# Two value products summed in one 32-row group, and row maxima written by GpSimd's DMAs, in a two-layer decoder kernel

## The reference

```
scores = jnp.einsum('bhqd,bhkd->bhqk', q, k) / np.sqrt(D).astype(np.float32)
scores = scores + bias[None]
scores = jnp.where(mask[None, None], scores, -jnp.inf)
wei = jax.nn.softmax(scores, axis=-1)
return jnp.einsum('bhqk,bhkd->bhqd', wei, v)
```

## Time and profile before

| | |
|---|---|
| median of 3 runs | 711.33 us (709.43 to 711.8) |
| profiled execution | 705.17 us, span 703.4 us |
| TensorE busy | 605.9 us, 86% |
| DVE, ACT, GpSimd busy | 562.7, 500.7, 319.2 us |
| chain that ended last | TensorE 55%, DVE 21%, issue 8%, GpSimd 6% |

### The profile page before, as it was taken

How to read it: one execution, slowest core, us unless ns; L and a number is a source line. 1 busy time by engine, 2 the same in 40 slices (tenths; PEclk the granted TensorE clock), 3 DMA queues, 4 the chain that set the end, 5 groups by cost and what they waited for, 6 DMA issues and landing times.

```text
span 703.4 us, 20504 instructions
## 1 busy us (share of the span) xinstructions
PE 605.9 (86%) x7396; PEld 362.6 (52%) x7396; DVE 562.7 (80%) x1551; ACT 500.7 (71%) x1229; POOL 319.2 (45%) x536
## 2 busy tenths in 40 slices
PE   0589899676677879999999989899999999999994
PEld 0256566444456658655454444455555555545663
DVE  5689988899999996878787777677777677678885
ACT  3689999977778746688888775577776766765531
POOL 3336765797899979865655311111211211101110
PEclk9999999988999989999999999999999999999998
DMA  6686974221111002444434426344354344330011
GB/s 229 142 170 157 251 114 85 53 66 46 38 39 38 32 3 40 76 77 78 77 76 78 82 59 104 70 86 76 62 92 78 61 92 77 54 52 19 32 38 38
DMA packets 162308, 55.18 MB, mean 78 GB/s; under 512 B 148448, under 2 KB 160032, under 8 KB 161952
## 3 DMA queue, kind: packets, MB, share of 16 engines
q1 hardware_dynamic: 162208, 53.88, 37.8%
HBM read 16.89 MB, written 5.24 MB: 31 GB/s over the span
## 4 chain that ended last, share of the span: by engine, by line
PE 55%; DVE 21%; issue 8%; POOL 6%; ACT 4%; DMA 4%; SPq 2%; DVEq 0%; ACTq 0%; POOLq 0%
PE bank L1330 5%; PE bank L1278 4%; PE bank L1264 3%; PE bank L999 3%; DVE l_neg_max L568 3%; PE bank L1679 3%; PE bank L1285 3%; DVE mix_num_den L1543 2%; PE bank L1303 2%; PE bank L1020 2%; DVE l1x_neg_max L1178 2%; PE bank L974 2%; PE bank L961 2%; PE bank L1356 2%; PE bank L1335 2%
## 5 line engine op out<-in xcount | busy, mean ns | idle before, releaser
L1178 DVE TENSOR_REDUCE l1x_neg_max<-bank 128x2 f16<-128x448 f32 (+1 forms) x192 | 116.0, 639 | 39.2 <-PE bank L1285 38.3
L1233 ACT ACTIVATE l1x_probs<-bank 128x512 f32<-128x512 f32 x192 | 104.3, 593 | 32.9 <-PE bank L1307 22.6
L886 DVE TENSOR_REDUCE l1a_neg_max<-bank 128x4 f16<-128x512 f32 x128 | 83.5, 676 | 18.8 <-PE bank L974 17.3
L934 ACT ACTIVATE l1a_probs<-bank 128x512 f32<-128x512 f32 x128 | 69.4, 593 | 18.2 <-PE bank L988 18.2
L1125 POOL TENSOR_TENSOR l1x_rstd<-l1x_var_eps,minus_half 128x1 f32<-128x1 f32 x16 | 8.8, 550 | 135.8 <-DVE l1x_var_eps L1154 135.8
L1679 PE MATMUL bank<-mix_xT_parts,w_ternary 128*128 128x256 f16 x384 | 49.9, 280 | 12.2 <-DVE mix_hidden L1561 11.6
L1679 PEld LDWEIGHTS bank<-mix_xT_parts,w_ternary 128*128 128x128 f16 x384 | 36.4, 100 | 24.6 <-DVE mix_hidden L1561 15.8
L568 DVE TENSOR_REDUCE l_neg_max<-bank 128x4 f16<-128x512 f32 x64 | 41.8, 674 | 4.7 <-PE bank L697 4.3
L1493 POOL TENSOR_TENSOR mix_hidden_parts<-mix_hidden,mix_hidden_parts 128x256 f16<-128x256 f32 x48 | 38.4, 810 | 6.0 <-ACT mix_hidden_parts L1624 5.8
L1751 POOL TENSOR_TENSOR moe_rstd<-moe_var_eps,minus_half 128x1 f32<-128x1 f32 x16 | 8.8, 549 | 62.6 <-DVE moe_var_eps L1769 62.6
L1624 ACT CAST mix_hidden_parts<-mix_hidden 128x256 f16<-128x256 f32 x48 | 19.2, 406 | 25.1 <-DVE mix_hidden L1561 25.0
(11 more groups left out here) (265 smaller groups left out, 1797.8 us busy)
## 6 DMA issues: line engine op xcount, KB each, us to landing
ctx_projected<-mix_ctx_projected SPq DMA_DIRECT2D x16, 192.0 KB, 2.0
l1x_ctx_projected<-ctx_projected SPq DMA_DIRECT2D x16, 160.0 KB, 2.5
...
```

Source lines behind the costliest of these rows:

```text
L886: dve.tensor_reduce(mm[:, 16 * j + 4 * s:16 * j + 4 * s + 4], b_s[c % 3][:].rearrange("p (r k) -> p r k", k=P), AX.X, ALU.max, negate=True ...
L934: act.activation(prob[:, c, :], b_st[c % 2][:], ACT.Exp).then_inc(s_exp, 1)
L1178: dve.tensor_reduce(mm[:, first:first + count], scores, AX.X, ALU.max, negate=True).then_inc(s_max, 1)
L1233: act.activation(prob[:, c, :], b_st[c % 2][:], ACT.Exp).then_inc(s_exp, 1)
```

## The change

In l1a and l1x the second value product of a block (c = 1) takes its 32 weight columns 16 columns earlier. The columns of each kv head are 8 values, a one and zeros, so with that shift the product leaves rows 0 to 15 of a group as they are and adds values and sum in rows 16 to 24. Both products thus accumulate in one bank: the first starts it, the second ends it. OE, T1 and T1b run once a block instead of twice; the reciprocal takes 32 elements a partition instead of 16, the product 256 instead of 128. The ring of copies has 2 slots instead of 4.

```diff
@@ l1x, TensorE (l1a alike)
             elif piece == "PV":
-                wait(pe, s_oe, b * 2 + c)
+                wait(pe, s_oe, b)
                 for x in range(4):
-                    pe.matmul(b_ot[32 * x:32 * x + 32, :], vs[:, b % 3, 4 * c + x, 0:32], prob[:, 6 * c + x, :],
-                              start=True, stop=False, skip_group_check=True)
+                    col = 64 * (4 * c + x) - 16 * c
+                    pe.matmul(b_ot[32 * x:32 * x + 32, :], v_flat[:, b % 3, col:col + 32], prob[:, 6 * c + x, :],
+                              start=c == 0, stop=False, skip_group_check=True)
             elif piece == "T1":
-                pe.wait_ge(s_oe, b * 2 + c + 1)
+                pe.wait_ge(s_oe, b + 1)
                 for r in range(4):
-                    ins = pe.transpose(b_tail[:, P * r:P * r + P], ots[:, 2 * bp + c, P * r:P * r + P], net.ident[:])
+                    ins = pe.transpose(b_tail[:, P * r:P * r + P], ots[:, bp, P * r:P * r + P], net.ident[:])
@@ ACT
             elif piece == "OE":
-                act.wait_ge(s_pv, b * 2 + c + 1)
-                act.copy(ots[:, 2 * bp + c, :], b_ot[:]).then_inc(s_oe, 1)
+                act.wait_ge(s_pv, 2 * (b + 1))
+                act.copy(ots[:, bp, :], b_ot[:]).then_inc(s_oe, 1)
```

In l1x the four DMAs of M move from SP's program to GpSimd's:

```diff
@@ sp_program
-            if piece == "M":
-                sp.wait_ge(s_mt, b + 1)
...
-                        sp.dma_start(dst, mt[r0:r0 + 8, :]).then_inc(s_md, 16)
@@ pool_program
+            elif piece == "M":
+                pool.wait_ge(s_mt, b + 1)
+                for j in range(2):
+                    for z in range(2):
+                        row, r0 = 64 * j + MROW, 16 * j + 8 * z
+                        dst = qt[row:row + 1, b % 3, :, 64 * z:64 * z + 64].rearrange("o (x u) q -> o x u q", u=2)
+                        pool.dma_start(dst, mt[r0:r0 + 8, :]).then_inc(s_md, 16)
```

The order tables are new in all five stages. For l1x on TensorE:

```diff
-        F5 S.4-2 T1.1-4 ST.2-3 S.5-2 F7 T4-4 ST.3-3 M-2 T5-4 S.0-1 ST.4-3 PV.0-3 ST.5-3 S.1-1 T1.0-3 S.2-1 ST.0-2
-        PV.1-3 S.3-1 ST.1-2"""),
+        S.4-2 F5 T1.0-4 S.5-2 ST.2-3 T4-4 F7 M-2 ST.3-3 T5-4 S.0-1 ST.4-3 PV.0-3 S.1-1 ST.5-3 S.2-1 ST.0-2 S.3-1
+        PV.1-3 ST.1-2"""),
```

More of the change, by code:

```diff
@@ L1234, in act_program @@
             elif piece == "OE":
-                act.wait_ge(s_pv, b * 2 + c + 1)
-                wait(act, s_t1, (b - 2) * 2 + c + 1)
-                act.copy(ots[:, 2 * bp + c, :], b_ot[:]).then_inc(s_oe, 1)
+                act.wait_ge(s_pv, 2 * (b + 1))
+                wait(act, s_t1, b - 1)
+                act.copy(ots[:, bp, :], b_ot[:]).then_inc(s_oe, 1)
             elif piece == "T4":
@@ L1334, in pe_program @@
                     late = prob[:, 6 * c + 4 + x % 2, 256 * (x // 2):256 * (x // 2) + 256]
-                    ins = pe.matmul(out, vs[:, b % 3, 4 * c + x, 32:64], late.rearrange("p (r q) -> p r q", r=4),
-                                    start=False, stop=True, skip_group_check=True)
+                    col = 64 * (4 * c + x) - 16 * c + 32
+                    ins = pe.matmul(out, v_flat[:, b % 3, col:col + 32], late.rearrange("p (r q) -> p r q", r=4),
+                                    start=False, stop=c == 1, skip_group_check=True)
                 ins.then_inc(s_pv, 1)
             elif piece == "T1":
-                pe.wait_ge(s_oe, b * 2 + c + 1)
-                wait(pe, s_t2, b * 4 + 2 * c)
-                if b == 0 and c == 0:
+                pe.wait_ge(s_oe, b + 1)
+                wait(pe, s_t2, 2 * b)
+                if b == 0:
                     take(pe, prev.left, 0)
-                if c == 0:
-                    wait(pe, s_x, b)
+                wait(pe, s_x, b)
                 for r in range(4):
-                    ins = pe.transpose(b_tail[:, P * r:P * r + P], ots[:, 2 * bp + c, P * r:P * r + P], net.ident[:])
+                    ins = pe.transpose(b_tail[:, P * r:P * r + P], ots[:, bp, P * r:P * r + P], net.ident[:])
                 ins.then_inc(s_t1, 1)
             elif piece == "T4":
-                pe.wait_ge(s_t2, 4 * (b + 1))
+                pe.wait_ge(s_t2, 2 * (b + 1))
                 for a in range(2):
```

178 lines of the change are left out of this document (96 added, 82 removed), and 19 rows, old and new, of the table TIMES.

## The result

| | before | after |
|---|---|---|
| median of 4 runs | 711.57 us (709.43 to 712.43) | 702.11 us (700.82 to 702.93) |
| profiled execution | 705.17 us, span 703.4 us | 701.63 us, span 699.8 us |
| TensorE busy | 605.9 us | 592.3 us |

A forecast was written before the change was run, and what follows sets the result against it. TensorE looked like the bound in l1a and l1x, but loops with DVE and ACT would turn its savings into waits. Terms 0 (l0, mix), 0 (l1a), -3.5 (overlaps), 0 (l1x), 0 (GpSimd) gave 707.8 us, band 703 to 712.

The forecast's parts named there:

- l1x: l1x alone: the removed T1 comes back as waits, net about 0, from -10 to +5 us over 12 blocks.
- The wait ahead of S.2: l1x on TensorE: 0.4 us waiting for DVE's reduction in place of T1, besides 0.59 us ahead of ST.0.
- 0 for l1a alone: l1a alone, ten blocks: no gain, from -6 to +2 us.
- the walk of the turn: One l1a block followed on ACT and DVE from M: closes at 8.35 us against 8.32 before.
- Overlaps: Where two stages overlap: two thirds of 5.4 us of freed transposes gained, -3.5 us, from 0 to -7.
- GpSimd's transfers: l1x maxima issued by GpSimd: 1.0 us for each of four, hidden, so price 0.
- The limit that was worked out: l1x, GpSimd's time per issue that stays hidden: up to 1.2 us for ST.0, 1.12 for the low parts.
- Rival B: GpSimd's transfers hold up ST.0 and the next transposes in l1x: at 1.4 us each, 724 us; chance 0.2.
- Rival A: l1a and l1x: TensorE's whole saving of 20.5 us shows, 691 us; chance 0.2.
- Rival C: The new order of mix is worse: +8 us, with the overlaps 716 us; chance 0.15.
- Rival D: l1a and l1x: second value products held until earlier ones drain, 3.2 us more, 711 us; counted within the forecast's band.
- the first stages: l0 and mix, work kept but pieces shuffled: 0, from -4 to +6 us.

The follow-up runs named there:

- the first two experiments: Changed kernel with four unused extra transposes a block in l1x: between ST.5 and S.2, 702.89 us; behind PV.1, 707.3 us.
- the fourth: Kernel before with the value products summed in one bank, but the order tables of before and maxima by SP: 710.41 us, ratio to before 1.0031.
- T1 twice: Changed kernel with the four transposes of T1 in l1a done twice: 704.93 us.
- the third kernel: Changed kernel with the four transfers of l1x's maxima issued by SP again instead of GpSimd: 701.73 us.
- eight issues: Changed kernel with the four transfers of l1x's maxima cut into eight of half the size, all issued by GpSimd: 720.86 us.
- the nine kernels: The changed kernel and the follow-ups that keep its new tables in l0, mix and l1a; last addition of mix between 298.76 and 302.22 us.

## Why the prediction was right or wrong

**l1x: right, and shown.** The turn stayed at 13.36 us, S.2 and ST.0 came where they were walked, and the first two experiments and the fourth show that the removed transposes were nearly free. The wait ahead of S.2 came in its size; the one ahead of ST.0 is 0.34 us and not 0.6, because the walk let S.2 end 0.40 us after its start, and its rows last 0.57 us. The busy share fell to 95%, not to 92%: TensorE's busy time fell by 3.9 us in twelve turns, 0.32 us each, and not by 12 x 0.64; that the neighbours overlap a T1 group, so that it counts for 0.45 us, makes up some 0.19 of these 0.32 us. The wait of 0.48 us ahead of M was missed. That the sum of the turn came out all the same is in that part luck.

**l1a: the step that failed.** It stands as "0 for l1a alone" and "the turn closes at 8.35 us". Measured were 8.04 us, and -3.6 us over eleven turns in the pair of profiles. Counted from M at 347.34 us in the changed kernel, ST.3 came at 2.48 us (walked 2.6), ST.0 at 4.14 (4.25), ST.1 at 5.71 (5.85), S.3 at 5.94 (6.15) and the next M at 8.04 (8.35). The step is the walk of the turn, a sum of small errors to one side, 0.12, 0.07 and 0.10 us among them, each for a gap that was taken to be there, and together they ate the whole gain. The claim that DVE has no gap from 3.3 to 8.27 us is wrong too: it idles 0.21 and 0.22 us ahead of two of its reductions. T1 twice shows what the walk had not seen: in the new order T1 and F7 fill the time from S.3 to M on TensorE, and there the removed group is worth 0.42 us a turn. In the old order leaving out a T1, with its OE and the split of DVE's work, costs 0.15 us (8.31 to 8.46 us). So what the change brought in l1a came with the new order, for which the sum had no gain.

**Overlaps: too large, and not shown.** Forecast -3.5 us, in the pair of profiles -2.2 and +0.7, so -1.5 us; and the -2.2 us did not come again in the third kernel. A gain at the overlaps is not shown.

**GpSimd's transfers: right, with the wrong price.** The issue took 0.58 us and not 1.0, and lay below SP's, which was used as the lower bound; the term of the sum stays 0. By the Trainium skill ("DMA: Bandwidth & Descriptors", section "Latency and other measured facts") software-generated transfers begin 0.4 us later; here they land after 2.0 us in the median, and SP's transfers of l1a's maxima, of twice the size, after 1.7 us, which agrees in direction. The limit that was worked out, 1.1 to 1.2 us for each of four, agrees with what eight issues show, but a delay at the limit is not hidden: it cost 19 us. Rival B, with its 1.4 us, is ruled out in this kernel, but its mechanism exists. **Rival A** falls: its turns of 12.5 and 7.7 us stand against 13.36 and 8.04. **Rival C**, a worse order of mix, shows its sign in the pair of profiles, for the first addition of l1a came at 318.36 us and not at 316.78. But in the nine kernels with that order it came between 315.05 and 318.41 us, at 316.5 in the mean, so the order of mix is not worse. **Rival D** falls: 256 products of L1330 took 604 ns each before and 605 after, and l1x kept its turn.

**The time.** The direction is right and the size is too small: -3.5 us forecast, -9.5 us measured, or -6.6 us in the one series where the third kernel stands for the changed one. Between the two profiled executions the difference is -3.5 us as forecast, but that agreement is luck. Its terms are +1.6 us for the first stages (forecast 0), -3.6 us for l1a (0) and -1.5 us for the overlaps and l1x (-3.5), and they only add up to the same. The other 6 us of the 9.5 are the distance of before's profile, 705.17 us, from its median, while the changed kernel's runs lie within 2.1 us. The pair that was profiled near its medians, the fourth and the third kernel, differs by 8.6 us in the spans and 8.7 us in the times, 7 us of it in l1a. Why some of the kernels spread more than others is not settled, nor which stretch was quick in the profile of before; no second one was taken.
